# Waits as instructions of their own in a four-engine pipeline (audio tower, 1 core)

## The reference, cut to what matters

```python
# 1. token pooling: windows of 8 times, softmax over a window, weighted sum -> h (128, 94, 64)
scores = einsum('bwkf,of->bwko', xp, w) + b
h = sum(xp * softmax(scores, axis=2), axis=2)
# 2. attention, 8 heads of rank 32, on layernorm(h)
scores = einsum('bhtr,bhur->bhtu', q, k) / sqrt(64)
h = h + einsum('bhtd,hde->bte', einsum('bhtu,bud->bhtd', softmax(scores), x), VO)
# 3. on layernorm(h): 4 heads x 4 experts of width 16, causal attention, softmax gates over the
#    experts, residual, layernorm, two small layers with masks, layernorm, gates over the heads
h = h + ffn(layernorm(h))
```

## Time and profile before

| | us |
|---|---|
| median of 3 executions | 1027.19 (1025.25 to 1032.36) |
| the profiled execution | 1028.16 |
| its span, first to last instruction | 1026.4 |
| TensorE busy | 928.4 (90%) |
| VectorE busy | 855.5 (83%) |
| GpSimd busy | 770.6 (75%) |
| ScalarE busy | 742.0 (72%) |

### The profile page before, as it was taken

One profiled execution on the slowest core, in us unless ns is written; L12 is line 12 of the kernel. 1 busy time (PEld: TensorE's weight loads), 2 busy tenths in 40 slices (PEclk: granted clock), 3 DMA queues, 4 the chain that ended last, 5 costly groups with the idle time before them and its releaser, 6 DMA issues.

```text
span 1026.4 us, 39079 instructions
## 1 busy us (share of the span) xinstructions
PE 928.4 (90%) x16312; PEld 608.0 (59%) x16312; DVE 855.5 (83%) x1867; ACT 742.0 (72%) x2295; POOL 770.6 (75%) x1152
## 2 busy tenths in 40 slices
PE   3688999999999999999999999999999999989710
PEld 3255566666676666666666666666666666656510
DVE  3445688899989999899999998999989999997742
ACT  0345788788878888788878887888878788876400
POOL 2331335489887888789878888788878888988896
PEclk9679899999999999999999999999999999999955
DMA  6201111011111111111011111111100000001000
GB/s 191 71 1 39 39 39 40 10 38 36 42 42 44 44 43 44 44 43 38 19 37 40 43 43 44 44 44 43 43 14 13 7 10 13 13 14 23 7 8 11
DMA packets 40927, 36.45 MB, mean 36 GB/s; under 512 B 27312, under 2 KB 30512, under 8 KB 40752
## 3 DMA queue, kind: packets, MB, share of 16 engines
q1 hardware_dynamic: 40656, 33.96, 11.9%
q0 software_dynamic: 96, 0.00, 0.0%
HBM read 25.08 MB, written 3.08 MB: 27 GB/s over the span
## 4 chain that ended last, share of the span: by engine, by line
PE 58%; DVE 31%; POOL 6%; ACT 2%; issue 1%; DMA 1%; SPq 0%; POOLq 0%; DVEq 0%; ACTq 0%
DVE pu L1445 8%; DVE mx L1442 7%; PE psum L685 7%; PE psum L695 7%; PE psum L774 7%; PE psum L703 4%; PE psum L723 4%; PE psum L800 3%; PE psum L789 3%; PE psum L606 3%; PE psum L627 3%; PE psum L619 3%; DVE ct L1453 2%; PE psum L677 2%; DVE xt L1358 2%; PE psum L759 2%
## 5 line engine op out<-in xcount | busy, mean ns | idle before, releaser
L1131 ACT ACTIVATE pu<-psum,mx 128x94 f32<-128x94 f32 x512 | 165.3, 357 | 15.6 <-DVE mx L1407 15.5
L1181 ACT ACTIVATE pT<-psum 96x512 f32<-96x512 f32 (+1 forms) x224 | 131.9, 603 | 53.0 <-PE psum L774 53.0
L464 POOL TENSOR_TENSOR pu<-pu,pr 128x752 f32<-128x752 f32 x96 | 137.4, 1445 | 21.0 <-DVE pr L1417 21.0
L501 POOL TENSOR_TENSOR st<-st,neg_half 128x12 f32<-128x12 f32 x64 | 145.5, 2273 | 5.0
L774 PE MATMUL psum<-ident_w,pu 128*96 128x128 f32 (+1 forms) x896 | 136.1, 282 | 1.4 <-ACT pu L1175 0.4
L774 PEld LDWEIGHTS psum<-ident_w,pu 128*96 128x96 f32 (+1 forms) x896 | 96.5, 135 | 55.3 <-issue 48.8
L1407 DVE TENSOR_REDUCE mx<-psum 128x8 f32<-128x752 f32 x96 | 89.9, 938 | 40.1 <-PE psum L685 39.9
L1445 DVE TENSOR_TENSOR pu<-psum,mx 128x1536 f32<-128x1536 f32 (+2 forms) x96 | 117.5, 1224 | 3.3
L1442 DVE TENSOR_REDUCE mx<-psum 128x16 f32<-128x1536 f32 (+2 forms) x96 | 115.0, 1198 | 3.5 <-PE psum L759 3.4
L800 PEld LDWEIGHTS psum<-gx,ct 128*128 128x128 f32 x768 | 92.9, 191 | 40.6 <-issue 34.1
L1131 ACT ACTIVATION_READ_ACCUMULATOR pu<-psum,mx 128x1 f32 x512 | 115.3, 225 | 0.0
(11 more groups left out here) (179 smaller groups left out, 2305.6 us busy)
## 6 DMA issues: line engine op xcount, KB each, us to landing
xs<-in_x SPq DMA_DIRECT2D x64, 375.0 KB, 3.8
vb<-va SPq DMA_DIRECT2D x32, 128.0 KB, 2.2
out_h<-ho SPq DMA_DIRECT2D x128, 16.0 KB, 1.4
out_h<-ho SPq DMA_DIRECT2D x128, 7.5 KB, 1.4
vc<-va SPq DMA_DIRECT2D x96, 16.0 KB, 1.9
gx<-in_L_ffn_gate_w SPq DMA_DIRECT2D x16, 0.2 KB
fc<-in_L_ffn_fc_w SPq DMA_DIRECT2D x12, 1.0 KB
fc<-in_L_ffn_fc_b SPq DMA_DIRECT2D x12, 0.1 KB
```

The lines of the kernel that those rows point to most:

```text
L464: pool.tensor_tensor(p, p, bcast(pr[:, j, :, :].rearrange("p a b -> p (a b)"), 2, NTOK), ALU.mult).then_inc(at_normed, 1)
L501: pool.tensor_tensor(st[:, k, 3, :], st[:, k, 2, :], neg_half[:, 0:NJ * NH], ALU.pow).then_inc(rstd, 1)
L1131: ins = act.activation(pu[:, j, par, hp, 0:NTOK], psum[:, (low, high)[par], NTOK * hp:NTOK * hp + NTOK], ACT.Exp, bias=mx[:, j, par, hp:hp ...
L1181: act.activation(pT3[j][:, f - (0, 4, 6)[i], :, :, :].rearrange("p e b t -> p (e b t)"), psum[0:rows, bank, :], ACT.Copy).then_inc(p_copie ...
```

## The change

In front of each step that has waits, `nop(nofuse=True)` is issued between the waits and the step's first instruction: an instruction of the engine's sequencer that does nothing and that is not merged with what follows. It takes the place of the step's first instruction as the carrier of the wait, so that the step's instructions carry none from outside. This is done in `quad` of PE (39 places), ACT (34), DVE (33) and POOL (20). Three of PE's stand before steps that have no wait at that point. Waits inside a step's function are as before, and so is all of SyncE. Steps that had no wait get none. The diff, cut to the places spoken of:

```diff
@@ GpSimd, quad
                     if exists(g - 6, NQUAD):
                         pool.wait_ge(fl_inv, 2 * g - 10)
+                        pool.nop(nofuse=True)
                         finish(g - 6, v % 2, (g - 6) // 2)
@@ TensorE, quad
                     if exists(g - 1, NQUAD):
                         pe.wait_ge(x_scaled, 3 * g)
                         if exists(g - 5, NQUAD):
                             pe.wait_ge(p_copied, 7 * g - 32)
                         elif exists(g, NQUAD) and (g) % 4 == 0:
                             pe.wait_ge(tok_shifted, ((g) // 4) + 1)
                         else:
                             pe.wait_ge(x_scaled, 3 * g - 1)
+                        pe.nop(nofuse=True)
                         pool_x(g - 1, 7)
...
                     if exists(g - 4, NQUAD):
                         pe.wait_ge(s_shifted0, 2 * g - 6)
+                        pe.nop(nofuse=True)
                         score3(v % 2, 1, 1)
@@ ScalarE, quad
                     if exists(g + 1, NQUAD):
                         act.wait_ge(at_mixed, g + 2)
+                        act.nop(nofuse=True)
                         copy_cT(1, 4)
                         copy_cT(2, 5)
@@ VectorE, quad
                     if exists(g - 4, NQUAD):
                         dve.wait_ge(at_out, g - 3)
+                        dve.nop(nofuse=True)
                         add_out(g - 4, 7)
                         dve.wait_ge(at_added, g - 3)
+                        dve.nop(nofuse=True)
                         stats3(g - 4)
                     if exists(g - 5, NQUAD):
                         dve.wait_ge(s_scored, 3 * g - 14)
+                        dve.nop(nofuse=True)
                         soft(g - 5, 0, 1)
```

102 lines of the change are left out of this document (added).

## The result

The changed kernel takes 1100.84 us (median of four, 1098.68 to 1102.14) against 1027.63: ratio 1.0704, 95% interval 1.0662 to 1.0746, or 72.3 us more. The forecast was 1042.

A forecast was written before the change was run, and what follows sets the result against it. PE holds 58% of the chain and DVE 31%, sharing the bound in the middle. Waits on the chain add 11.7 us and further lateness 3.0, together 14.7, taking the median from 1027.19 to 1042; range 1034 to 1056.

The forecast's parts named there:

- Duration of the new instruction: On every engine, the same as an existing semaphore instruction: 51 ns on PE, 0.02 us on ACT, POOL and DVE.
- A satisfied wait costs nothing: Where the wait was over long before, the sequencer passes it while the engine still works: cost 0.
- Prices of a passage: Where the engine stands at a chain wait, now separate: +0.075 us on DVE, +0.08 POOL, +0.06 ACT, +0.10 PE.
- The middle, 27.55 us a group: From 190 to 900 us, a group grows from 27.17 us by 0.25 at add_out, stats3, pool_x and 0.125 of further lateness.
- knock-on: PE's late second and third score3 delay DVE's soft steps: 0.125 us a group, 3 us over some 24 groups.
- Start and tail: Waits on the chain cost 3.3 us from 12 to 130 us and 2.7 us from 900 us on.
- busy times stay: Sign expected in the new profile: the engines' busy times do not change.
- upper rival (1083): Every wait pays on PE: 34.6 instructions a group at 51 ns, 1.8 us a group, 56 in all; chance 0.07.
- Hidden: Few waits bind and sequencers work ahead: sum 4 to 10 us, 1031 to 1037, say 1034; chance 0.16.
- Faster: PE's first weight load, without a carried wait, loses its 0.2 us idle ahead of a step: 65 us, 962; chance 0.03.
- The chain's idle time becomes 0.10, 0.10 and 0.14: Sign expected in the new profile: idle us on the chain at add_out, stats3 and pool_x, new instruction included.
- add_out starts 27.5 to 27.6 us apart: Sign expected in the new profile: group length in the middle; staying at 27.2 would mean these waits did not bind.

The follow-up runs named there:

- after_single: The changed kernel with mask_hidden and head_shift's subtraction replaced by VectorE instructions that read one SBUF operand; 1053.24 us, ratio 1.0226.
- before_single: The kernel before with mask_hidden and head_shift's subtraction replaced by VectorE instructions that read one SBUF operand; 1026.11 us, ratio 0.998.
- after_fill: The changed kernel with six unused matmuls on PE ahead of pool_x's wait in three groups of four; 1085.77 us, ratio 1.0560.
- before_one: The kernel before with one separate wait a group, in front of VectorE's mask_hidden; 1029.93 us, ratio 1.000.
- only_act: The kernel before with the separate waits on ScalarE (ACT) alone; 1034.93 us, ratio 1.0065.
- only_pe: The kernel before with the separate waits on TensorE (PE) alone; 1070.33 us, ratio 1.0442.

## Why the prediction was wrong

By the ratios the 72.3 us divide into three:

| part | from | us |
|---|---|---|
| the separate waits themselves | after_single less before_single: 23.2 + 2.1 | 25.3 |
| DVE held by GpSimd | after_fill less after_single, less what before gains: 57.5 - 23.2 - 2.1 | 32.2 |
| PE's clock in the middle | changed kernel less after_fill: 72.3 - 57.5 | 14.8 |

Each is a difference of two ratios and uncertain by some 3 to 5 us. The filling of after_fill also touches other steps, so the last two parts are less sharply divided than their sum.

**Duration of the new instruction: right** (51 ns on PE, 21 on DVE, 17 on ACT and POOL). Their number was too high: the pages count 3235 more instructions in place of 3702, because a step with two waits had a semaphore instruction already, and one such instruction holds both. Nothing hung on it.

**A satisfied wait costs nothing: right.** before_one, only_act's groups, and PE's 31.17 for 31.10 us, which is less than one passage for some 35 waits. The load ahead of `give_out` idles 0.2 us at most, as in the earlier trace rows.

**Prices of a passage: right where they were measured.** +0.070 (said 0.075) at `stats3`, +0.091 (0.10) at `pool_x`; those of ACT and POOL were not measured by themselves.

**The middle, 27.55 us a group: right where nothing is held.** after_single has 27.61 against 27.18 in its control, 0.43 against the 0.375 forecast. The knock-on is where the prediction put it: the third soft starts 10.58 us behind `add_out` for 10.39, its neighbour, the subtraction of the second soft, only 0.085 later; so 0.10 came in between. The matmuls of the third `score3` end 0.15 later by their modelled ends.

**Start and tail: too small.** 3.3 us were priced up to 130 us and 2.7 for the tail. The control pair has 9.1 up to the first `add_out` alone and 2.4 + 3.8 from the 28th on; with the middle it has 25.3 for the 14.7 priced. The prediction counted passages at a fixed speed of PE, while the granted clock there fell from 0.82 to 0.71. How much of the 9.1 is the clock and how much is passages was not separated. That ACT and GpSimd don't matter in the middle was right for ACT, wrong for GpSimd (0.13 us a group, by way of L1502).

**The step that failed: "busy times stay".** In its place the runs showed `mask_hidden` held by GpSimd, 1.4 to 2.0 us instead of 0.36 in 17 of 32 groups (32.2 us, with the longer subtraction of `head_shift`), and behind that PE's clock at half (14.8 us). I moved starts and kept every duration from the trace of before, and asked of each late step only who waits for it. Not asked was what runs beside it. Two instructions of different engines with no wait between them, 70 ns apart, were treated as independent. The trace of before had the warning in one line: L1488 with 361 ns in the median and 1956 at the longest, and the two long ones (at 811.5 and 974.5 us) are those that start 188 and 126 ns behind `head_mul`, against 68 to 80 for the others that start behind it. A flip of 20 such instructions at 1.6 us each would have been a rival of 32 us, and the idle time on PE behind it would have raised the question of the clock. The upper rival (1083) had nearly the size and a mechanism that only_pe refutes; Hidden falls with the 25.3 us, and Faster with the load ahead of `give_out`, which idles as before.

**The forecast marks.** "The chain's idle time becomes 0.10, 0.10 and 0.14": it is 0.09, 0.09 and 0.14. "add_out starts 27.5 to 27.6 us apart": only in after_single; in the changed kernel 29.2, or 30.8 where the clock falls (32.5 where it falls for 6.8 us).

No version here beats the kernel before. With the waits and without the holds it is 2.3% slower; without either it is not measurably faster, since PE is busy 26.95 of 27.2 us.

## What to carry to other kernels

Before a change that shifts engines by tens of ns is priced, look for instructions whose longest duration is far from their median, find what runs beside the long ones, and note the distance at which they turn: such a pair has a cliff, and the change needs only to reach it. On VectorE this concerns instructions with two SBUF operands that run beside GpSimd's; keep them apart by order, or read one operand from elsewhere. And where TensorE is the bound, an idle time of 2 us can cost almost as much again in clock (1.6 us, behind 19 of 31 in two kernels here, but behind 6 of 52 that were up to 1.9 us long in three others); matmuls that nobody needs can be cheaper than standing.

## What was not expected of the hardware

The order of the two engines is not that of their recorded starts. In the twelve profiled kernels that have `head_mul` and `mask_hidden` in their old form and order, 227 `mask_hidden` start while `head_mul` runs. DVE went first in all that started up to 76 ns behind `head_mul`, both outcomes occur from 77 to 87 ns, and from 88 ns on DVE was held every time. The Trainium skill (SBUF — State Buffer, "SBUF: two separate sides") gives the lock to whoever starts first; by the recorded starts this is off by some 80 ns in DVE's favour.

When DVE goes first, GpSimd's `head_mul` takes 0.3 us more; when GpSimd does, DVE loses 1.6 us. The sum of both engines' lost time is thus five times larger the wrong way round.

The clock of TensorE fell to half for 3.4 us (twice 6.8) behind idle times of 2.0 us, in an engine that was otherwise busy 93% of the group. Six matmuls without use in each such gap kept it at 1.00 through the middle.
